# A graph network with four layers on one core: fewer TensorE signals, and GpSimd's DMA issues without pauses or waits for TensorE between them

## What is computed

```python
edge_index = jnp.stack([src, dst])
x = _layernorm(x + L0(x, edge_index, W1l, b1l, W1r, W2l, b2l, W2r))   # two dense layers on the mean of the neighbours
x = _layernorm(x + L1(x, edge_weight, Wn, bn, Ws, bs, src, dst))      # three hops: H = A_w @ H @ Wn.T + bn + H @ Ws.T + bs
x = _layernorm(x + L2(x, W1, W2, b, src, dst))                        # t1[src] + (x[src] * x[dst]) @ W2, scaled, summed, normed
x = _layernorm(x + L3(x, edge_index, W, att_src, att_dst, ...))       # attention with 8 heads
...
# L3, the last layer
h = (x @ W).reshape(n, HEADS, OUT_DIM)
e = jax.nn.leaky_relu(a_src[src] + a_dst[dst], NEG_SLOPE)
e = jnp.exp(e - jax.ops.segment_max(e, dst, num_segments=n)[dst])
alpha = e / (jax.ops.segment_sum(e, dst, num_segments=n)[dst] + 1e-16)
out = jax.ops.segment_sum(h[src] * alpha[:, :, None], dst, num_segments=n)
```

## Time and profile before

| | us |
|---|---|
| median of 3 runs | 2978.43 (2973.93 to 2991.66) |
| the profiled execution | 2951.49 |
| its span | 2949.3 |
| TensorE busy | 2292.1 (78%) |
| VectorE busy | 1474.2 (50%) |
| GpSimd busy | 1003.7 (34%) |
| ScalarE busy | 660.9 (22%) |

### The profile page before, as it was taken

How to read it: one execution, slowest core, us unless ns; L and a number is a source line. 1 busy time by engine, 2 the same in 40 slices (tenths; PEclk the granted TensorE clock), 3 DMA queues, 4 the chain that set the end, 5 groups by cost and what they waited for, 6 DMA issues and landing times.

```text
span 2949.3 us, 30712 instructions
## 1 busy us (share of the span) xinstructions
PE 2292.1 (78%) x8708; PEld 1530.2 (52%) x8708; DVE 1474.2 (50%) x4063; ACT 660.9 (22%) x1371; POOL 1003.7 (34%) x1317
## 2 busy tenths in 40 slices
PE   4677788998887999999999999999933545554550
PEld 2444788344665555565556555577722434343340
DVE  8999665454674001061103501455543747574778
ACT  3777645111443000010001000255500000000002
POOL 0000266666666000000000000000138788878740
PEclk8888899998999999999999999999965666665675
DMA  6565688443344544455444534333333333333321
GB/s 241 244 251 225 212 249 256 129 141 99 99 125 160 143 152 131 152 167 189 131 152 163 178 120 147 91 107 102 93 69 101 90 98 101 98 89 99 88 60 44
DMA packets 191910, 411.94 MB, mean 140 GB/s; under 512 B 47735, under 2 KB 131410, under 8 KB 191762
## 3 DMA queue, kind: packets, MB, share of 16 engines
q1 hardware_dynamic: 128276, 240.65, 26.5%
q10 hardware_dynamic: 27325, 102.15, 9.8%
q0 software_dynamic: 36160, 67.34, 8.6%
HBM read 326.06 MB, written 83.96 MB: 139 GB/s over the span
## 4 chain that ended last, share of the span: by engine, by line
PE 62%; DVE 23%; another core or an unknown queue 5%; issue 5%; DMA 2%; ACT 1%; POOL 1%; ACTq 0%; DVEq 0%; SPq 0%; POOLq 0%
PE banks L1528 28%; PE banks L950 8%; PE banks L2382 7%; DVE features_and_rows L566 6%; PE banks L1208 3%; PE banks L1193 3%; PE banks L1076 3%; PE banks L1515 2%; PE banks L1498 2%; DVE pair_and_bias_rows L563 2%; PE banks L1968 1%; DVE row_ring L2351 1%; POOL row_ring L2160 1%; DVE features_and_rows L1256 1%
## 5 line engine op out<-in xcount | busy, mean ns | idle before, releaser
L790 POOL DMA_INDIRECT table_dense_weights<-pair_weight,dst x416 | 412.3, 991 | 551.3 <-DVE weights_c L845 321.2
L1528 PE MATMUL banks<-own_term,features_and_rows 128*128 128x391 f32 (+1 forms) x1656 | 552.3, 491 | 0.0
L2160 POOL DMA_INDIRECT row_ring<-table_heads,src x416 | 411.6, 989 | 115.4 <-issue 65.6
L1528 PEld LDWEIGHTS banks<-own_term,features_and_rows 128*128 128x128 f32 x1656 | 312.2, 189 | 226.8
L2382 PE MATMUL banks<-row_ring,edge_to_window 128*128 x880 | 277.7, 481 | 109.8 <-DVE edge_to_window L2357 97.7
L950 PE MATMUL banks<-split_rows,count_columns 128*128 128x512 f32 x1200 | 316.7, 410 | 19.6 <-ACT count_columns L932 11.0
L1554 DVE TENSOR_SCALAR features_and_rows<-banks,hop_bias 128x391 f32<-128x391 f32 (+1 forms) x24 | 15.0, 625 | 609.0 <-PE banks L1528 609.0
L2382 PEld LDWEIGHTS banks<-row_ring,edge_to_window 128*128 128x128 f32 x880 | 199.9, 235 | 185.1 <-issue 136.6
L1528 PE MATMUL banks<-features_and_rows 128*128 128x391 f32 (+1 forms) x840 | 282.4, 491 | 0.0
L950 PEld LDWEIGHTS banks<-split_rows,count_columns 128*128 128x128 f32 x1200 | 223.1, 190 | 75.1 <-ACT count_columns L932 14.3
L584 PE MATMUL banks<-features_and_rows,pair_and_bias_rows 128*128 128x400 f16 x806 | 183.1, 386 | 86.8 <-DVE features_and_rows L566 51.7
(11 more groups left out here) (422 smaller groups left out, 2927.1 us busy)
## 6 DMA issues: line engine op xcount, KB each, us to landing
hidden<-table_counts SPq DMA_DIRECT2D x305, 160.0 KB
table_dense_weights<-weights_c ACTq DMA_DIRECT2D x26, 1600.0 KB, 5.7
own_term<-table_dense_weights SPq DMA_DIRECT2D x52, 782.0 KB
own_term<-table_dense_weights SPq DMA_DIRECT2D x34, 780.5 KB
pair_and_bias_rows<-table_edge_rows ACTq DMA_DIRECT2D x50, 512.0 KB
weights_c<-table_edge_rows ACTq DMA_DIRECT2D x50, 512.0 KB
features_and_rows<-table_dense_weights SPq DMA_DIRECT2D x26, 782.0 KB
table_counts<-hidden SPq DMA_DIRECT2D x25, 800.0 KB, 3.4
```

Source lines behind the costliest of these rows:

```text
L790: e.indirect_dma_start(out=self.table, out_offset=bass.IndirectOffsetOnAxis(ap=self.place[:, t:t + 1], axis=0), in_=self.values[:, t:t + 1 ...
L1528: m = e.matmul(psum[b][:, 0:wide], z_block(block)[:, f * P:(f + 1) * P], streamed[tile % STREAM][:, lo - from_column:lo - from_column + wi ...
L2160: e.indirect_dma_start(out=ring_rows[:, ring_at(t), 0:ATT_ROW], out_offset=None, in_=t_h, in_offset=bass.IndirectOffsetOnAxis(ap=src[:, t: ...
```

## The change

TensorE's operations signal in groups: `T` has an argument `last`, and with `last=False` the operation goes to the list without an increment (`pr.part`). So do all but the last transpose or matmul of a group: the turns of the attention's scores, maxima, weights and start rows, the transposes of node tiles, the matmuls of a bank in the dense layers. A merge step increments `s_mm` only when it is the fourth of its quad; the waits count quads, and the computed step at which a node tile ends is shifted right by two. In the first two passes `s_a_used` is incremented after groups 2 and 4 only (`USED_AT`), and ScalarE's widening of a group waits for the next of these.

On GpSimd the pause behind each gather and `multiplied_beside` ahead of the scatters are gone, with the numbers that set its places.

```diff
+    def part(self, e, fn, *waits):
+
+        waits = [w for w in waits if w is not None]
+
+        def emit(eng):
+            for s, v in waits:
+                eng.wait_ge(s, v)
+            fn(eng)
+
+        self.queue[e].append(emit)
...
-        def pause(e):
-
-            if paused[0]:
-                e.wait_ge(s_paused, paused[0])
-            e.iota(spare_count[:, :], [[1, PAUSE]], base=0, channel_multiplier=0).then_inc(s_paused, 1)
-            paused[0] += 1
-
         V = lambda fn, *w: pr.op("dve", fn, *w)
         A = lambda fn, *w: pr.op("act", fn, *w)
-        T = lambda fn, *w: pr.op("pe", fn, *w)
+        T = lambda fn, *w, last=True: pr.op("pe", fn, *w) if last else pr.part("pe", fn, *w)
...
             def step(self, e, s):
-                multiplied_beside(e, 2 * s)
-                self.tiles(e, s, 0, 2 * s)
+                self.tiles(e, s, 0)
                 if s > 1:
                     self.in_memory(e, s - 2)
                 if s:
-                    multiplied_beside(e, 2 * s + 1)
-                    self.rest(e, s - 1, 2 * s + 1)
+                    self.rest(e, s - 1)
...
-        dense_layers_from, turned_from = [0], [0]
-        IN_ROWS, IN_LAYERS, IN_SECOND, IN_TURNS, IN_HOPS = 8, 29, 66, 99, 101
-
-        def multiplied_beside(e, half_step, half=0):
-            if IN_ROWS <= half_step < IN_LAYERS:
-                e.wait_ge(s_a_used, min(45 + 4 * (half_step - IN_ROWS) + 2 * half, of_group(Q1, 0) + NODE_TILES * COUNT_GROUPS - 1))
-            elif IN_LAYERS <= half_step < IN_SECOND:
-                e.wait_ge(pr.done["pe"], dense_layers_from[0] + max(1, 6 * (half_step - IN_LAYERS) - 10 + 3 * half))
...
+        USED_AT = (COUNT_GROUPS // 2, COUNT_GROUPS - 1)
+        used = lambda q, g: q * len(USED_AT) + (1 if g <= USED_AT[0] else 2) if q < Q3 else of_group(q - Q3, g) + Q3 * len(USED_AT)
...
                 e.wait_ge(*a_landed(q, g))
-                    e.wait_ge(s_a_used, of_group(q - 1, g))
+                    e.wait_ge(s_a_used, used(q - 1, g))
                 e.copy(in_group(count_columns, g), in_group(slot_of(q), g)).then_inc(s_a_wide, 1)
...
-                m.then_inc(s_a_used, 1)
+                if g in USED_AT:
+                    m.then_inc(s_a_used, 1)
...
-                          freed if q == 0 else None, scaled[c], xt_ready if q == 0 else None, l_w)
+                          freed if q == 0 else None, scaled[c], xt_ready if q == 0 else None, l_w, last=q == len(pairs) - 1)
...
-        V(lambda e: e.tensor_scalar(merge_control[0:1, MERGE_STEPS:], ends_at, float(UNROLL), None, ALU.add), (s_merge, 1))
+        ends_known = V(lambda e: e.tensor_scalar(merge_control[0:1, MERGE_STEPS:], ends_at, float(UNROLL * GROUP + GROUP - 1), None, ALU.add), (s_merge, 1))
+        V(lambda e: e.tensor_scalar(merge_control[0:1, MERGE_STEPS:], merge_control[0:1, MERGE_STEPS:], 2, None, ALU.arith_shift_right),
+          ends_known)
...
-        merged = lambda tile: (s_mm, mm0 + tile + NODE_TILES)
+        merged = lambda tile: (s_mm, mm0 + -(-(tile + NODE_TILES) // GROUP))
...
-                    pause(e)
...
             for i in range(SCAN_TILES):
-                m = T(lambda e, i=i: e.transpose(of_tiles(weight_of, i), gap[:, i * P:(i + 1) * P], ident[:, :]), t)
+                m = T(lambda e, i=i: e.transpose(of_tiles(weight_of, i), gap[:, i * P:(i + 1) * P], ident[:, :]), t, last=i == SCAN_TILES - 1)
...
             if quad >= 2:
-                e.wait_ge(s_mm, quad * GROUP + (mm0 - GROUP))
+                e.wait_ge(s_mm, quad + (mm0 - 1))
...
-                e.matmul(banks[:, bass.ds(column_at, RING_ROW)], onehot[:, s % UNROLL, :], ring[:, bass.ds(row_at, RING_ROW)],
-                         start=False, stop=False, skip_group_check=True).then_inc(s_mm, 1)
+                m = e.matmul(banks[:, bass.ds(column_at, RING_ROW)], onehot[:, s % UNROLL, :], ring[:, bass.ds(row_at, RING_ROW)],
+                             start=False, stop=False, skip_group_check=True)
+                if s % GROUP == GROUP - 1:
+                    m.then_inc(s_mm, 1)
```

More of the change, by code:

```diff
@@ L782, in __init__, with tiles @@
                 self.steps = pr.sem(f"{name}_steps_in_memory")
-            def tiles(self, e, s, c, half_step=0):
-                for i, k in enumerate(range(c, UNROLL, 3) if s < THIRDS else range(c, UNROLL, 2)):
+            def tiles(self, e, s, c):
+                for k in range(c, UNROLL, 3) if s < THIRDS else range(c, UNROLL, 2):
                     t = s * UNROLL + k
-                    if i == 2:
-                        multiplied_beside(e, half_step, 1)
                     self.count[c][s % 2] += 16
@@ L791, in tiles, with rest @@
                                          in_=self.values[:, t:t + 1], in_offset=None).then_inc(self.landed[c][s % 2], 16)
-            def rest(self, e, s, half_step=0):
+            def rest(self, e, s):
                 e.wait_ge(self.landed[0][s % 2], self.count[0][s % 2])
-                self.tiles(e, s, 1, half_step)
+                self.tiles(e, s, 1)
                 if s < THIRDS:
@@ L1005, in run @@
                 m = multiply_rows(e, psum[0], lambda k: count_columns[:, k, :], (k,), 0, True)
[L1006 removed]
+                if k % COUNT_GROUP == COUNT_GROUP - 1 and k // COUNT_GROUP in USED_AT:
                     m.then_inc(s_a_used, 1)
@@ L1020, in residual_gnn @@
                     m = T(lambda e, i=i, j=j, k=k: e.transpose(psum[i][:, k * P:(k + 1) * P], x[:, j, k * P:(k + 1) * P], ident[:, :]),
-                          turned_x.get(j - 3) or counts_kept)
+                          turned_x.get(j - 3) or counts_kept, last=k == K_IN - 1)
                 turned_x[j] = xt_ready = A(lambda e, i=i, j=j: e.copy(
@@ L1163, in running_sum @@
             before = lambda n: ps[:, n * 32:n * 32 + NODE_TILES]
-            T(lambda e: e.matmul(before(0), triangle, counts, start=True, stop=True), freed, tri)
+            T(lambda e: e.matmul(before(0), triangle, counts, start=True, stop=True), freed, tri, last=False)
             m = T(lambda e: e.matmul(before(1), ones[:, :], counts, start=True, stop=True))
@@ L1209, in from_hidden @@
                                                                        w_b[:, mt, :], start=(mt == 0), stop=(mt == K_HID - 1)),
-                          freed if mt == 0 else None, made[c])
+                          freed if mt == 0 else None, made[c], last=mt == K_HID - 1)
                 hid_read[c % 2] = m
@@ L1216, in from_hidden @@
                                               split_of[j], xb)
-        dense_layers_from[0] = pr.count[pr.done["pe"].name]
         to_hidden(0)
@@ L1295, in turn0 @@
                     m = T(lambda e, ps=ps, j=j, k=k: e.transpose(ps[:, k * P:(k + 1) * P], x[:, j, k * P:(k + 1) * P], ident[:, :]),
-                          freed, t)
+                          freed, t, last=k == K_IN - 1)
                 reader[i] = A(lambda e, ps=ps, j=j: e.copy(xT[:, :, j * P:(j + 1) * P],
@@ L1305, in residual_gnn @@
         V(lambda e: e.reciprocal(rdeg[:, :], rdeg[:, :]), d2)
-        turned_from[0] = pr.count[pr.done["pe"].name]
         in_groups(turn0)
@@ L1827, in residual_gnn @@
                 m = T(lambda e, ps=ps, j=j, k=k: e.transpose(ps[:, k * P:(k + 1) * P], xT[:, k, j * P:(j + 1) * P], ident[:, :]),
-                      freed, *hops_done)
+                      freed, *hops_done, last=k == K_IN - 1)
             turned_late[j] = i, ps, m
@@ L2272, in turn_start @@
                         start_values[b % 2][:, i, :, c], ident[:, :]),
-                        (s_start[b % 2], 16 * (b // 2 + 1)), held_read.get(b - 1))
+                        (s_start[b % 2], 16 * (b // 2 + 1)), held_read.get(b - 1), last=c == 1 and i == SCAN_TILES - 1)
             for w in range(2):
                 keys_spread[b] = T(lambda e, w=w: e.matmul(keys_of[:, w * P:(w + 1) * P], end_key[:, b, w:w + 1].broadcast_to([P, P]),
-                                                           ident[:, :], start=True, stop=True), keyed_ends, max_read.get(b - 1))
+                                                           ident[:, :], start=True, stop=True), keyed_ends, max_read.get(b - 1), last=w == 1)
         def prepare(b):
@@ L2314, in weigh @@
                 m = T(lambda e, w=w, at=at: e.matmul(end_values[:, w * P:(w + 1) * P], back[:, at:at + 1].broadcast_to([P, P]), ident[:, :],
-                                                     start=True, stop=True), spread_max)
+                                                     start=True, stop=True), spread_max, last=w == 1)
             t = V(lambda e: e.tensor_tensor(at_ends, end_mask, all_values.unsqueeze(1).broadcast_to([P, 2, ALL_KEYS]), ALU.add),
```

26 lines of the change are left out of this document (9 added, 17 removed).

## The result

The changed kernel takes 3254.02 us (median of 4 runs, 3242.14 to 3260.57) against 2976.18 for the kernel before on the same chips: a ratio of 1.092, 95% interval 1.087 to 1.098. The profiled execution has a span of 3256.7 us, 307.4 more than before. TensorE's busy time hardly moved (2341.6 us for 2292.1), and its share fell from 78% to 72%.

The account below looks back on a forecast made before the run. It took TensorE as the bound from 331 to 936 us, and gathers plus queued TensorE signals in the attention. 2951.5 - 85 - 43 + 2 = 2825.5, plus 26.9 for the median: 2852 us; own range 2802 to 2895, 8-in-10 range 2795 to 3035.

Parts of the forecast that it names:

- What bounds the kernel now: Attention: gathers nearly bound it, 51 us lost mainly to ring rows; TensorE's signals queue, about one per DMA GpSimd issues.
- (1) Fewer signals: Attention: 46 TensorE signals per part become 14, needing 18 us, so no pile forms; remote waits shrink to about 1 us each.
- (2) Own rate: Attention: unpaced gathers take 1.29 us each, the last 540 us after the first, parts 41.3 us; -85 us.
- (3) Scatter stages: First pass, dense layers, second pass: thinner signals let TensorE's gaps close and scatters run closer; -43 us.
- (4) Coarser waits: First two passes and merge: later widening and evictions hide under other work; nothing to +6 us, +2 in the sum.
- (B): Slower: unpaced GpSimd leaves signals less room; parts 58 us, passes +50 less 20, 3120 us; weak form 52, 3018; chance 0.23.
- (A): Attention: signals late because GpSimd issues, not because many; each handoff 1.5 us late, -42, scatter stages -10, 2926 us; chance 0.18.
- What a signal costs: Merge: the skill's 26.3 ns per increment makes 330 saved signals worth 9 us; set against 5.75 us per four signals.

Follow-up runs that it names:

- thin_paced: The changed kernel with the pause of 128 after each gather and the waits for TensorE between scatters put back: 2972.1 us, ratio 1.001 to the kernel before.
- thin_pause_192_192: The changed kernel with a pause of 192 numbers behind each scatter and each gather, no waits for TensorE between scatters: 2854.5 us, ratio 0.963.
- thin_paced_192: thin_paced with the pause behind each gather at 192 numbers instead of 128: 2935.6 us, ratio 0.989.

## Why the prediction was wrong

Two steps failed. The 5.75 us per quad were taken for a rate of signals, so that fewer signals would free the gaps; and on this ground the pause and the waits between scatters were counted as a cost to be saved (-85, and part of -43), while they were what kept TensorE going (+0.021 and +0.071).

**What bounds the kernel now** held in its facts: TensorE's work was done and its signal late; how much GpSimd issues decides. The inference failed that "TensorE's signals get through at about one per DMA". The 1.44 us came from dividing 5.75 by four signals; thin_paced has the 5.7 us with one signal (shown). The trace of before could have told it. TensorE's merges of three quads there:

```profile
2405.46 8.57 PE L2382 MATMUL banks<-row_ring,edge_to_window 128*128 x24 [0.90 <-DVE edge_to_window L2357]
```

The last of the three quads is merged at 2414.03, and the one-hots two quads behind it start at 2421.90, 7.9 us later: one late signal, which two quads in flight share. A smaller misreading: of GpSimd's 115.4 us idle before gathers 12.1 stand before the first one, so it waited 37.7 us for ring rows and not 51; the rest of the 51 is gathers that last longer than the typical 0.95 us.

**(1) Fewer signals.** "On this reading no pile forms": the waits are as before, 126.1 us for 124.7. The term carried the attention's -85 and most of the -43, and measures 0.001 of the time, an interval of -4 to +11 us.

**(2) Own rate.** The period was right, 1.27 us from start to start. That gathers then end 540 us after the first was wrong, 692 measured: the merge frees ring rows too late, and GpSimd waits 124.4 us for them. In 1.27 us only 0.3 are free of an issue, and VectorE's remote waits are 177.9 us, where 0.42 of 1.38 gave 124.7. Parts start (3127.57 - 2474.86) / 12 = 54.4 us apart, not 41.3.

**(3) Scatter stages.** Forecast -43, measured +242 ahead of the attention. I looked for what closes TensorE's gaps, and took a run of scatters as free if nothing waits on them. The gain itself is there when the pacing leaves room: 70 us ahead of the attention in thin_pause_192_192.

**(4) Coarser waits** cost nothing, as taken (thin_paced).

**The rivals.** (B) came nearest: without the pauses signals get through worse, and parts of 54.4 us lie between its weak 52 and its 58. Its price ahead of the attention, 1 us a tile or +30 in all, was off by 212 us; so even its 3120 fell short, and 3254 lies outside every range that I had given. The earlier trace rows hinted at it: the wait of 8.66 us ended while GpSimd had stopped, so a run that doesn't stop may hold it on. The chance of 0.23 for slower was too low with 46 signals becoming 14 as the only argument against, an argument that rested on the same division. That the attention fell between its two sizes is in part luck: 58 was the mean of two parts and 52 a weaker guess, neither worked out from what a pause leaves free. (A) had the better half of the cause, that signals are late because GpSimd issues, with too small a price.

**What a signal costs.** The Trainium skill has an increment cost 26.3 ns ("TensorE: Matmul & The Clock Gate", "The cost: per-tile semaphore tail"), an estimated 9 us for 330. I set it aside for rows 7. The runs lie nearer to it than to my -85 us, and show even less: thin_paced is -4 to +11 us from the kernel before. Its saving needn't be on the path, so they don't measure the 26.3 ns.

**What stays open.** What exactly is held while GpSimd issues: the trace shows TensorE's matmuls starting 1.4 to 3.5 us apart and its signals late, but not the resource. Gathers with fewer rows, to tell the issue from the transfer, weren't tried.

## What to carry to other kernels

A long loop of indirect DMAs issued by GpSimd back to back isn't free for the other engines, even if nobody waits for it: look for remote waits and for matmuls that start far apart with "issue" between them, and give GpSimd a short job between two issues. Here the pause's length was worth 7 points (1.036 at 128, 0.963 at 192 in both places), and a scan over three lengths finds the edge. Before a rate is built on one ratio, vary its divisor, and look how many rounds are in flight: a delay that two quads share looks like a rate. One signal per quad in place of four, with the pacing left in, would have told it in one run.

## Unexpected of the hardware

With GpSimd issuing an indirect DMA every 1.27 us (0.97 of it the issue) in an unbroken run of 65 us, TensorE's matmuls of 0.38 us started 1.4 to 3.5 us apart from its eighth microsecond on, and ScalarE waited 62 us, for some 57 of which nothing that it needed was still under way. At one gather per 1.38 us a signal came up to 13.1 us late; at one per 1.46 us waits were up to 4.6 us in one trace (thin_paced_192) and not remote in another (thin_pause_192_192); at one per 1.52 no wait of VectorE's was remote. The first two figures are of typical neighbours and the last two means; in the mean, without waits, the first two are an estimated 1.28 (0.977 + 0.30) and 1.41, so the whole effect comes and goes within 0.2 us. The pauses are GpSimd's own work (0.26 us for 128 numbers, 0.36 for 256): in thin_pause_192_192 GpSimd is busy 537 of 608 us of the attention, in the changed kernel 407 of 691. So a busy GpSimd isn't the cause; the issuing is, or what the issued DMA does.
